# Four-layer graph network on one core: own rows added on TensorE in the second attention hop, joined row loads in the mean layer

## What is computed

```python
agg = segment_sum(edge_weight * x[dst], src)
out = concat([agg, x]) @ W.T
x = layernorm(x + relu(layernorm(out) * gamma + beta))
```

```python
def agg(x):
    e = leaky(sum((concat([x[head], x[tail]]) @ fc_w.T + fc_b) * rel_e))
    ex = exp(e - segment_max(e, head)[head])
    w = ex / segment_sum(ex, head)[head]
    return segment_sum(x[tail] * w, head) + x
for _ in range(2):
    x = agg(x)
    x = x / maximum(norm(x), 1e-12)
x = layernorm(x_in + x)
```

## Time and profile before

| | |
|---|---|
| three executions | 6962.48, 6962.85, 6965.23 us (median 6962.85) |
| profiled execution | 6984.61 us, of it 6982.7 us span |
| granted clock of PE over the span | 0.933 of full speed |

### The profile page before, as it was taken

The page is one execution under the profiler, slowest core; times in us unless marked ns, Lnnn a source line. Parts: engine busy times, 40 slices in busy tenths (PEclk is TensorE's granted clock), DMA queues, the critical chain, the costliest instruction groups (busy, mean ns, idle before and its releaser), DMA issues. The chain is left out here.

```text
span 6982.7 us, 169103 instructions
## 1 busy us (share of the span) xinstructions
PE 6298.9 (90%) x37102; PEld 5098.3 (73%) x37103; DVE 5285.4 (76%) x18168; ACT 4280.0 (61%) x14748; POOL 3904.1 (56%) x3592
## 2 busy tenths in 40 slices
PE   5676899997789998989999899999899998999999
PEld 2222788886688887769999788888566666888887
DVE  9887888887655654247777677777688887899998
ACT  0000899995214443238888677777588787677777
POOL 6677777775736666754444444444444444444443
PEclk9555999998879999999999899999899999999999
DMA  1200666666656666667777666665577676444443
GB/s 40 6 2 8 182 193 193 194 194 192 182 154 192 199 197 186 198 186 222 222 222 222 178 185 187 186 187 173 176 221 216 205 221 184 123 126 127 128 127 118
DMA packets 1224976, 1161.36 MB, mean 166 GB/s; under 512 B 314483, under 2 KB 1152523, under 8 KB 1224094
## 3 DMA queue, kind: packets, MB, share of 16 engines
q1 hardware_dynamic: 1067230, 943.02, 43.9%
q0 software_dynamic: 157632, 217.06, 13.3%
HBM read 946.93 MB, written 395.69 MB: 192 GB/s over the span
## 5 line engine op out<-in xcount | busy, mean ns | idle before, releaser
L215 POOL DMA_INDIRECT l_gathered<-x,by_dst_meta x384 | 433.6, 1129 | 547.7 <-PE l_ps_a L1571 485.8
L1836 POOL DMA_INDIRECT l2b_gathered<-z,by_src_meta x408 | 431.1, 1057 | 534.9 <-PE l2b_ps_g L2079 419.6
L1836 POOL DMA_INDIRECT l2a_gathered<-x,by_src_meta x408 | 431.1, 1057 | 453.8 <-PE l2a_ps_g L2079 338.1
L215 POOL DMA_INDIRECT l1b_gathered<-messages,by_dst_meta x384 | 395.3, 1029 | 437.8 <-PE l1b_ps_b L1434 376.8
L215 POOL DMA_INDIRECT l1a_gathered<-messages,by_dst_meta x384 | 432.1, 1125 | 206.7 <-PE l1a_ps_b L1434 141.7
L700 PE MATMUL l2b_ps_x<-zero_row,ones_b 128*128 128x392 bf16 x2912 | 510.1, 330 | 0.0
L215 POOL DMA_INDIRECT l_gathered<-in_x,by_src_meta x384 | 417.7, 1088 | 130.7 <-issue 113.9
L889 PE MATMUL l_ps_b<-l_w,l_x_t 128*128 128x256 f32 x1592 | 416.2, 384 | 38.8 <-DMA l_x_t<-in_x_turned 37.8
L865 ACT ACT_TABLE_LOAD x1 | 1.3, 1283 | 702.6 <-PEq L129 702.6
L1432 PE MATMUL l1b_ps_b<-root,l1b_x_t 128*128 128x256 f32 x1600 | 425.8, 389 | 0.0
L1432 PE MATMUL l1a_ps_b<-root,l1a_x_t 128*128 128x256 f32 x1584 | 415.6, 385 | 3.8 <-DVE l1a_hot L670 1.6
(11 more groups left out here) (402 smaller groups left out, 20682.5 us busy)
## 6 DMA issues: line engine op xcount, KB each, us to landing
x<-l1b_result SPq DMA_DIRECT2D x400, 152.0 KB, 3.0
z<-l2a_result SPq DMA_DIRECT2D x400, 152.0 KB
l2a_x<-x SPq DMA_DIRECT2D x53, 1024.0 KB
l2b_x<-z SPq DMA_DIRECT2D x53, 1024.0 KB
l1b_x<-h SPq DMA_DIRECT2D x408, 128.0 KB
l1b_res<-x SPq DMA_DIRECT2D x408, 128.0 KB
l2b_res<-x SPq DMA_DIRECT2D x51, 1024.0 KB
l_x_t<-in_x_turned SPq DMA_DIRECT2D x406, 128.0 KB
```

The lines of the kernel that those rows point to most:

```text
L215: pool.indirect_dma_start(gathered[:, slot, 0:D], None, source[0:count, :], bass.IndirectOffsetOnAxis(ap=rows, axis=0), bounds_check=limit ...
L1836: pool.indirect_dma_start(gathered[:, k, :], None, x_in[0:N_NODES, :], bass.IndirectOffsetOnAxis(ap=rows, axis=0), bounds_check=limit, oob ...
```

## The change

**Second hop only.** DVE's `divide` and `add_self` go. A new DVE step `weigh_own` (o+1), first in the round, waits for all eight chances of its octet, forms `own_share` (the item's share of the denominator, gated so that padding adds nothing), writes a diagonal matrix of it for each item (`diagonal`, 128 x 1024, one instruction), scans the denominator with `own_share` and prepares a least value `least` for the norm's guard. On PE every item of `aggregate` gets a second matmul into the same bank, diagonal times own rows x, with x chosen by a register; the first of them waits for `diagonal`. So `agg` (now 16 slots) holds the running s + d * x, `measure` squares it, `have_square` guards by `least`, and `add_residual` reads `agg` instead of y. DVE's list has a new order, PE's first fill has 24 instead of 48 matmuls, and PE has a second register load (`find_own`). SP's load of own rows waits for PE's `x_added` instead of DVE's `y`.

**Mean layer.** The host lays x and its turned tile side by side (`x_both`, rows of 512). SP loads both with one transfer of 256 KB for each item, 16 slots deep, again when the item is `summed`; it loads registers twice for 8 items. All engines' loops go by 16 items in a body, `load_hops` bodies, instead of 8 items and `load_groups` bodies; `gather_rows` runs for `load_hops * 2` groups.

```diff
-    groups = load_groups(pool, graph)
+    groups = load_hops(pool, graph) * 2 if wide else load_groups(pool, graph)
...
+    hops = load_hops(eng, graph)
+    for n in range(-max(ahead for _, ahead in steps), 0):
+        for step, ahead in steps:
+            if n + ahead >= 0:
+                step(WidePair(0, n + ahead))
+    with eng.Fori(0, hops) as g:
+        for n in range(RING):
+            for step, ahead in steps:
+                step(WidePair(g, n + ahead))
...
+        both = ph.sb("both", [P, HOP, 2 * D], F32)
+        x, x_t = both[:, :, 0:D], both[:, :, D:2 * D]
...
+                def load(row, slot):
+                    sp.dma_start(both[:, slot, :], x_both[bass.ds(row, P), :]).then_inc(in_both[slot], 16)
...
+                with sp.Fori(0, hops) as g:
+                    for half in range(2):
+                        first = g * HOP + half * RING
+                        rows = rows_of(store_regs, STORE, first)
+                        next_rows = rows_of(load_regs, LOAD, first + HOP)
+                        for k in range(RING):
+                            sp.wait_ge(s["summed"], first + (k + 1))
+                            load(next_rows[k], half * RING + k)
+                            sp.wait_ge(s["out_ready"], first + (k + 1))
+                            sp.dma_start(x_out[bass.ds(rows[k], P), :], result[:, k, :]).then_inc(s["stored"][k], 16)
...
-                        sp.wait_ge(s["y"], octet.item - OCT)
+                        sp.wait_ge(s["x_added"] if last_hop else s["y"], octet.item - OCT)
...
+                def weigh_own(o):
+                    pass_wait(dve, s, s["shrunk"], o.number + 1)
+                    pass_wait(dve, s, s["chance"], o.item + OCT)
+                    dve.scalar_tensor_tensor(own_share[:, o.both], below[:, o.half, :], -FLOOR, share[:, o.both], ALU.is_ge, ALU.add)\
+                        .then_inc(s["own_share"], 1)
+                    o.wait(dve, s["own_share"])
+                    if o.after(1):
+                        pass_wait(dve, s, s["x_added"], o.item)
+                    dve.tensor_tensor(diagonal[:], c.ident[:].unsqueeze(1).broadcast_to([P, OCT, P]),
+                                      own_share[:, o.both].unsqueeze(2).broadcast_to([P, OCT, P]), ALU.mult)\
+                        .then_inc(s["diagonal"], 1)
+                    before = (o.base - 1) % HOP
+                    if o.after(1):
+                        dve.wait_ge(s["den"], o.number)
+                    dve.tensor_tensor_scan(denom[:, o.both], shrink[:, o.half, :], own_share[:, o.both],
+                                           denom[:, before:before + 1], ALU.mult, ALU.add).then_inc(s["den"], 1)
+                    o.wait(dve, s["den"])
+                    dve.scalar_tensor_tensor(least[:, o.both], denom[:, o.both], TINY, denom[:, o.both], ALU.mult, ALU.mult)\
+                        .then_inc(s["least"], 1)
...
+                    pass_wait(dve, s, s["out_ready"], o.item + (ready_from - OCT))
                     for j, k in o.each():
-                        dve.scalar_tensor_tensor(y[:, k, :], y[:, k, :], inv.root[:, k:k + 1], res[:, bass.ds(at[k % OCT], 1), :],
+                        dve.wait_ge(s["agg"], j + 2)
+                        dve.scalar_tensor_tensor(y[:, k, :], agg[:, k, :], inv.root[:, k:k + 1], res[:, bass.ds(at[k % OCT], 1), :],
...
-                    steps = [(add_residual, 0), (find_slots, 1), (scores, 2), (divide, 1), (part(add_up, 0), 1), (centre, 0), (part(add_up, 1), 1),
-                             (part(add_self, 0), 1), (part(add_self, 1), 1), (have_variance, 0), (maximum, 2), (have_square, 1),
-                             (find_nodes, 3), (lambda o: inv2.square(dve, o), 0), (lambda o: inv2.weigh(dve, o), 0),
+                    steps = [(weigh_own, 1), (add_residual, 0), (centre, 0), (scores, 2), (find_slots, 1), (find_nodes, 3),
+                             (part(add_up, 0), 1), (part(add_up, 1), 1), (have_variance, 0), (maximum, 2), (have_square, 1),
+                             (lambda o: inv2.square(dve, o), 0), (lambda o: inv2.weigh(dve, o), 0),
...
-                        pe.matmul(ps_g[:, k % OCT, :], hot[:, k % OCT, :], gathered[:, k, 0:D], start=True, stop=True)\
+                        pe.matmul(ps_g[:, k % OCT, :], hot[:, k % OCT, :], gathered[:, k, 0:D], start=True, stop=not last_hop)\
                             .then_inc(s["agg_done"], 1)
+                        if last_hop:
+                            pe.matmul(ps_g[:, k % OCT, :], diagonal[:, k % OCT, :],
+                                      x[:, bass.ds(at[k % OCT] + o.base, 1), :].rearrange("p k d -> p (k d)"), start=False, stop=True)\
+                                .then_inc(s["x_added"], 1)
...
-                    steps = [(find_slots, 3)] + [(part(aggregate, n), 1) for n in range(4)] + [
-                        (spread, 2), (part(fill, 48), 2), (part(turn_chances, 0), 2), (part(fill, 4), 2),
+                    steps = [(part(aggregate, n), 1) for n in range(4)] + [
+                        (spread, 2), (find_own, 2), (find_slots, 3), (part(fill, 24), 2), (part(turn_chances, 0), 2), (part(fill, 4), 2),
                         (part(turn_chances, 1), 2), (look_up, 3), (part(fill, 4), 2)]
```

More of the change, by code:

```diff
@@ L694, in wait_items, with __init__, each_wide @@
         eng.wait_ge(sem, self.item + 2)
+class WidePair(Pair):
+    def __init__(self, group, n):
+        super().__init__(group * 2, n)
+        self.wide = 2 * n % HOP
+        self.wide_lap = group + n // RING
+    def each_wide(self):
+        return [(self.item + q, self.slot + q, self.wide + q) for q in range(2)]
 def keep_busy(pe, c, spare, n):
@@ L805, in between @@
                             sources.send(SOURCES_BEFORE + n - EC)
[L807 removed]
+                gather_rows(pool, graph, s, index, gathered, x_in, extra=2, between=between, wide=True)
                 by_dst.finish()
@@ L1710, in attention_hop @@
         share, denom, guarded, inverse, total_sq = (ph.sb(k, [P, HOP], F32) for k in ("share", "denom", "guarded", "inverse", "total_sq"))
-        squares = ph.sb("squares", [P, OCT, D], F32)
+        rooms = 4 if last_hop else OCT
+        squares = ph.sb("squares", [P, rooms, D], F32)
         restart = ph.sb("restart", [P, ITEMS], F32)
-        res = ph.sb("res", [P, OCT, D], F32) if last_hop else None
+        if last_hop:
+            res = ph.sb("res", [P, OCT, D], F32)
+            own_share, least = ph.sb("own_share", [P, HOP], F32), ph.sb("least", [P, HOP], F32)
+            diagonal = ph.sb("diagonal", [P, OCT, P], F32)
         def load_slots(eng, regs, octet):
@@ L2015, in measure @@
                 def measure(o, first, n):
-                    for j, k in o.each()[first:first + n]:
-                        act.wait_ge(s["y"], j + 1)
-                        act.activation(squares[:, k % OCT, :], y[:, k, :], ACT.Square, accum_out=total_sq[:, k:k + 1])\
+                    for q, (j, k) in enumerate(o.each()[first:first + n]):
+                        if last_hop:
+                            act.wait_ge(s["agg"], j + 2)
+                            if q >= rooms:
+                                act.wait_ge(s["squared"], j - 3)
+                        else:
+                            act.wait_ge(s["y"], j + 1)
+                        act.activation(squares[:, k % rooms, :], (agg if last_hop else y)[:, k, :], ACT.Square, accum_out=total_sq[:, k:k + 1])\
                             .then_inc(s["squared"], 1)
@@ L2071, in aggregate @@
                 def aggregate(o, n):
+                    if last_hop:
+                        at = slots_of(pe, own_regs)
+                        if n == 0:
+                            o.wait(pe, s["diagonal"])
+                            pe.wait_ge(in_x[o.half], (o.lap + 1) * 16)
                     if n % 2 == 0:
```

84 lines of the change are left out of this document (55 added, 29 removed).

## The result

| | before | changed |
|---|---|---|
| median (us) | 6962.73 (4 runs, 6962.48 to 6965.23) | 7036.59 (4 runs, 7027.80 to 7040.93) |
| ratio | | 1.0104, 95% interval 1.0086 to 1.0121 |
| profiled execution, span (us) | 6982.7 | 7039.2 |
| granted clock | 0.933 | 0.931 |

The change costs 74 us. The forecast was 7080 us, the range 7000 to 7145; the time fell on rival 1 (7035 us).

The account below looks back on a forecast made before the run. DVE's list after the last chance, with PE's clock loss every second round, bounds the hop: (21.4 - 19.16) x 50 = +112 us, mean layer +4, hop start +1; median 7080 us, range 7000 to 7145.

Parts of the forecast that it names:

- rival 1: Second hop: DVE's chain sets rounds of 20.45 to 20.8 us without PE clock loss; +72, 7035 us; chance 0.20.
- The bound of the hop: Second hop: DVE's list from the last chance to the maximum takes 14.5 us, giving a round of 20.45 us.
- W: Second hop: the end of an octet's last chance on ACT, from which the round's steps are counted.
- The load without cover: Second hop, DVE: `find_slots`' register load of 0.596 us, now behind `score`, takes 1.2 us with three waits.
- The clock: Second hop, PE: a 2.6 us gap lowers the clock every second round, about 22.4 us; mean round 21.4.
- The mean layer: Mean layer: SP no longer bounds, POOL's pairs stay at 4.70 us; sum about +4 us, bounds -33 to +17.
- The rounding: Mean layer: 49 groups of 8 become 25 of 16, four more pairs on PE's path, 17.4 us.
- Rival 4: Second hop: maximum waits for PE's `spread` at 12.8 us after the last chance; round 18.75, -20 us, 6948 us; chance 0.09.

Follow-up runs that it names:

- nodes_back_b: Changed kernel with `find_nodes` put back behind the maximum, where before takes about 6963 to 6970 us; 6967.77 us, 0.9995 of before.
- slots_nofill: Changed kernel with `find_nodes` behind the maximum, `find_slots` right behind `add_residual`, and no four fills ahead of PE's aggregation; 6940.43 us, 0.9955 of before.
- the hop alone: Kernel before with only the second hop's part of the change; 7040.95 us against 6970.05, ratio 1.0107.
- fill32: Changed kernel with 32 instead of 24 filling matmuls in PE's first fill; 7050.97 us, 1.0114 of before.
- weigh_later: Changed kernel with `weigh_own` behind `add_residual` and `centre` instead of ahead of them; 7078.15 us, 1.0151 of before.
- mean_tail: Kernel before with only the mean layer's change, but 24 bodies plus half a body written out, so no rounding to 50 groups; 6953.94 us, 0.9975 of before.
- the mean layer alone: Kernel before with only the mean layer's part of the change; 6962.58 us against 6970.05, ratio 0.9992.
- nodes_slots: Changed kernel with `find_nodes` behind the maximum and `find_slots` right behind `add_residual`, on the chip where before takes 7831.61 us; 1.0165 of before.
- best28: Changed kernel with `find_nodes` behind the maximum, `find_slots` behind `add_residual`, no four fills before aggregation, 28 first fills for 24; 6932.96 us, 0.9949 of before.

## Why the prediction was right, and where it was off

**The bound of the hop.** Right. The prediction has "Maximum at W + 14.5" and a round of 20.45: measured W + 14.3 and W + 14.7 in turn, 20.47 us. Step by step, forecast and the two kinds of round: diagonal from 0.55 (0.48, 0.55); its length 1.21 (1.23); `add_residual` from 2.7 (2.6, 2.9); `scores` from 6.45 (6.3, 6.7); `find_nodes` from 8.8 (8.7, 9.3); `add_up` from 10.3 (10.2, 10.6). The load without cover cost 1.1 to 1.3 us with its waits, against 1.2; the waits ahead of `add_residual` differ with the octet, which makes the two kinds of round. Two experiments give the list's price, the second not by itself: 1.5 us less in the list, 1.5 us less in the round (`nodes_back_b`); another 0.9 us less, with four fills less on PE, and the round falls by 0.7, to 18.3 (`slots_nofill`).

**The clock.** The step that failed, and the only one that kept the forecast at 7080. For every second round I had "start W + 5.6, 7.2 us of full-speed work of which 2 to 4 us are at half speed", from the earlier trace rows, where the low level lasted over most of the aggregation. That the clock would fall after a gap of over 2 us, in every second round, was right: 0.96 from 5100 to 5800 where it is 1.00 with more fills. But the low spell is about 3.4 us long in all 25 rounds that have one, and covers no more than the eight transposes and the fills between them; the aggregation starts at W + 4.15 at full speed, its `spread` is done at W + 13.3, and DVE gets there at 14.3. The term mis-sized is the length of the spell: 3.4 us against the 10 that I carried over from the longer of the two spells in the trace of before (the other lasted 6.8 us, in a round of 21.69). A spell of 10.2 us and the round of 22.5 that I forecast do exist, in 2 of 25 such rounds of the hop alone, so what was wrong is how often; what decides the length is open. The granted clock in the hop was 0.96, not 0.8 to 0.9. With short spells, 50 rounds of 20.47 give (20.47 - 19.16) x 50 = +66 us, rival 1's number. That the whole time comes within 2 us of rival 1's 7035 is in part luck: rival 1 has +5 beside its hop, and what was measured there is -3, +5 and +9, of which the last two were not forecast. I gave that rival 0.20 and called its gaps harmless; they do lower the clock, and `fill32` shows that this is free, since PE has the slack. The Trainium skill's page "TensorE: Matmul & The Clock Gate", section "HAM oscillation", has a kernel pay the loss in every pass; the low level recurs here too, in each second round, but the runs show that it is paid only where PE is the one waited for (`weigh_later`, the five rounds of `slots_nofill`, the two long spells of the hop alone), which is for the waits to tell and not for the rule.

**The mean layer.** Forecast +4 us (-33 to +17), measured -3 in the trace and 0.9992 (0.9983 to 1.0002) alone. The rounding's 17.4 us is confirmed. What pays for it is the join: without the rounding (`mean_tail`) the layer's last result begins at 1640.8, with before's loads at 1659.5 (before) and 1658.2 (the hop alone), so the join is worth 17 to 19 us and the rounding takes 17.4 back. The -3 itself is no more than executions differ by, as the mean layer alone has 1658.2 too, and the other kernels with the same layer 1654.4 to 1662.9. Nor is POOL shown to be faster by the change: its 184 pairs took 1562.37 - 705.5 = 856.9 us, in before 1567.38 - 705.63 = 861.8, and in the hop alone, with before's layer, 859.4. The prediction's 865.4 us up to 1571.07 held 185 pairs and not 184, 4.68 us each and not 4.70; nothing in its sum hangs on the difference.

**Rival 4** (faster, PE sets the round, W + 12.8 needed) had its point where I put it: with the maximum at W + 13.0 in the mean the time equals before (`nodes_back_b`), with 12.3 and 11.9 in turn it is below (`slots_nofill`). Its mechanism, the maximum waiting for `spread`, is not what was seen: also there DVE came last, by 0.2 us, except in the rounds with a lowered clock. The change had put 1.3 us too much behind the chances for it.

**Not forecast:** 9 us in the last layer, below.

## What to carry to other kernels

When a step is added that must wait for an engine's last result and stands first in a list, everything behind it loses its cover; count that list from the wait to the next handover, waits and register loads included, and move out of it what has another place in the loop. That count was good to 0.1 us in 20 here, and the 4.1 us of DVE work taken out per octet did not make up for what lost its cover. A lowered TensorE clock is to be priced by who waits for TensorE while it lasts, not by its presence: a loss of 3.4 us was free in one order of the steps and cost 1.7 us a round or more in another, and in the first order too it cost 2 us in the two rounds in which it lasted 10 us.

## What the runs showed of the hardware

**Instructions that come late.** On the chip of the first four runs, which none of the others fell on, the kernel before took 7831.61 us. The expectations on record there:

> The kernel before with the change in the mean layer alone (joined transfers, bodies of 16 items). In the trace of the changed kernel this layer ended at 1657.2 us against 1660.1 before, with four pairs more. Theory 1 (the hop makes the whole difference): 6960 us, ratio 0.9996, so 3 us less than before, and the last layer takes its 1059 us. Theory 2 (the mean layer's change moves something elsewhere, as the last layer, 9.4 us longer in the changed kernel): 6970 us.

> The kernel before with the change in the second hop alone. Theory 1: the hop takes 64 us more, as in the changed kernel (20.49 us per round against 19.16), 7027 to 7037 us. Theory 2 (part of the cost lies in the mean layer or comes from both together): under 7020 us.

> The changed kernel with find_nodes put back behind the maximum and have_square. Theory 1 (the round is the vector engine's list from the last chance to the maximum): the list gets 1.5 us shorter in one round and 1.2 at least in the other, the maximum comes 13.0 to 13.3 us after the last chance, the round is 19.1 to 19.3 us, and the time 6975 us. PE's gap before the turned chances falls from 2.95 to about 1.3 us and its clock stays full. Theory 2 (PE's lost clock in every second round is what the hop pays for): the clock comes back too, so time is the same, but rounds that had no clock loss before (20.72 us) would not get shorter than 20.3. Theory 3 (ACT sets the round, since its squares end only 14.9 us after the last chance): no gain, 7030 us.

> As nodes_back, and the register load find_slots is put right behind add_residual instead of behind the score. Theory 1: the load of 0.6 us runs under the last additions; the maximum comes 12.5 to 12.8 us after the last chance, just behind PE's spread (12.3), the round is 18.5 to 18.7 us and the time 6945 us, less than before. Theory 2 (the load isn't covered there, since the instructions ahead still use its registers): as nodes_back, 6975 us. Theory 3 (PE or ACT takes over): between the two, with the maximum waiting for the scores on PE.

Measured, as ratios to before on that chip: the mean layer alone 0.9813 (0.9797 to 0.9830), the hop alone 1.0360 (1.0337 to 1.0382), `nodes_back` 1.0185 (1.0168 to 1.0202), `nodes_slots` 1.0165 (1.0143 to 1.0187). DVE in the hop alone, and the waits of 700 us of it:

```profile
6235.90 0.17 DVE L2017 TENSOR_SCALAR l2b_inv_v<-l2b_norm_squares 128x8 f32<-128x8 f32 x1
6241.89 1.23 DVE L1971 TENSOR_REDUCE l2b_peak<-l2b_ps_e 128x8 f32<-128x1024 f32 x1 [5.82 <-DMA l1b_res<-x]
```

```profile
DVE l2b_peak L1971 <- DMA l1b_res<-x: 131.6, 25, 6.1
...
PEld l2b_ps_x L700 <- issue: 41.7, 130, 1.3
```

The scores on PE were done at 6235.1; the maximum waited until 6241.89, and the name that the profile puts there is a buffer of a layer long past, so nothing of this phase released it. The stall is there once in each round, at the same step, and PE stops for its own fills, which wait for nothing. On the other chips the maximum follows within 0.1 us. It looks like late code: the Trainium skill's page "Runtime: NRT & Kernel Launch", section "Instruction fetch mechanics", says that a taken branch to code not at hand has to wait for a fetch. The trace has no record of such fetches, so this is argued and not shown; and since a pass over the loop holds two rounds and each of them has the stall, the branch at the loop's end would not be enough to explain it. That chip prices the two halves otherwise: rounds of the hop are 26.7 to 27.1 us for all three orders of DVE's list ((7034.6 - 5650.1) / 51 = 27.1 in the hop alone), so the list rules less there; in the mean layer, where before's SP was saturated, the join is worth 160 us (last result at 1713 against 1873).

**The last layer has two speeds.** Its code is the same in all kernels, and eight of its items took 20.6 to 20.7 us (median) in before and in each half alone, and 20.8 to 21.0 in the changed kernel and in all the other variants, `mean_tail` among them; over 360 items that is 930 to 934 against 939 to 944 us, +9 in the changed kernel. Nothing in its input or its orders differs. What decides is open; since `mean_tail` and the mean layer alone differ only in code ahead of it, where its instructions lie is a candidate, not tried.

**The clock can fall without a gap that shows.** Idle times of 1.50 us ahead of the transposes left it alone in every second round of the changed kernel, and with none over 0.2 us (`best28`) it fell. The length of the idle time alone does not tell.
